# First attention: layout change of the outputs by transfers through DRAM in place of TensorE

## The chip, the cores and the metric
One NeuronCore of a Trainium2 chip runs the whole program, and the metric is the device time of one execution in microseconds (us). The engines are TensorE (PE; its weight loads are shown as PEld), VectorE (DVE), ScalarE (ACT), GpSimd (POOL) and SyncE (SP), which here issues transfers. Every engine works through its own queue in order. Engines meet only at semaphores. SP and ACT each have a DMA queue of their own; both feed the same 16 DMA engines.

## The reference, cut to what matters
The input is 16 sequences of 512 tokens with 128 channels. The network is: a mixture-of-experts block, softmax attention, the same mixture-of-experts block again, a second (kernel-feature) attention, and a spline block. The change touches the softmax attention alone, which for 16 heads of 8 channels computes

```
qkv  = x @ qkv_w + qkv_b                     # x is layer-normalised, 512 x 128
attn = softmax(q k^T / sqrt(8))              # 16 heads, 512 x 512 each
out  = (attn @ v) laid out as 512 x 128      # heads side by side
out  = out @ proj_w + proj_b                 # added to the residual
```

## The kernel before, in words
The program runs in stages with a barrier between them: set-up, `ffnA`, `att` (function `attn0`, the one changed), `ffnB`, another set-up, `att1k`, `att1q`. In `att` one sequence is a **batch** (16 batches). A batch has four **units** of four heads, and 32 **steps**, each of which handles one unit, one tile of 128 tokens and one pair of heads.

Every engine's program is a double loop: `m` over batches (18 turns, since work on a batch ends two turns after its scores began), and `n` over the 32 steps. What an engine does in step `n` stands in order in that loop. In each step TensorE does `again` (line 957: the scores of a step 42 steps back once more, transposed, with the row maxima folded in, two matmuls of 512 columns), `scores` (line 947: the scores of the next step, two matmuls), and on most steps `weigh` (line 969: eight matmuls of 256 columns by 32 columns of values, which accumulate in bank `o`). DVE takes the maxima of `scores` (line 698), ACT takes the exponential of `again` (line 873). Three double banks `pair` are handed round: `again` waits in `pair_free` for a maximum 1.5 steps old, `scores` for the exponential of the step before. The `scores` and `again` matmuls of one step lie on different rows of the array and can run at once.

Around that, one bank `misc` serves everything that is done once or a few times a batch, always in the order of `uses_of_misc`, each use waiting until the last one was read: the turned maxima, the turned input, the projections of queries, keys and values, and the outputs.

How the outputs leave. The values have a ninth column of ones, so a unit's bank `o` holds, for each of four heads, 8 rows of weighted sums and one row of softmax sums, tokens along the columns, in blocks of 32 rows. ACT copies it (`out`, line 879). TensorE turns it back (`turn_back`, line 117: four transposes into `misc`). DVE inverts the sums (line 720) and multiplies (line 722) into `otok`, which has tokens on partitions and heads side by side. When all four units of a batch are there, TensorE turns `otok` (`final`, line 111), ACT copies it to `ocol` (line 885), TensorE projects it (`projected`, line 993) and DVE adds it to the residual (`ended`, line 727). In turn `m` the units 2 and 3 of batch `m - 2` come at PE steps 7 and 15, `final` at 21, `projected` at 23, units 0 and 1 of batch `m - 1` at 25 and 30.

SP moves queries and keys to their spread layout through DRAM: `operands(m + 1)` waits until POOL has split the query into two parts (lines 770, 772), issues three writes (line 800), waits for them, reads 1 MB back (line 810), then does the same for the keys (line 816). Before that, in the same turn, `maxima(m - 1)` writes and reads the row maxima (lines 822, 825). POOL normalises a batch (lines 148, 154), adds the bias (line 786) and splits queries and keys, in that order, batch by batch.

Of the kernel before, what the change touches and what calls it, by code (L numbers as in the profile page):

```python
# [15 lines left out]
P = 128  # L16
# [549 lines left out]
HALF = 256  # L566
WEIGHED = {4: ((0, 0),), 5: ((0, 1),), 6: ((1, 0),), 7: ((1, 1),), 8: ((2, 0),), 9: ((2, 1), (3, 0)), 10: ((3, 1),)}
# [7 lines left out]
def attn0(nc, ctx, name, X, A, K, groups):  # L575
# [12 lines left out]
    (var, root, normed, biased, xT, xc, qp, kp, qr, kr, ql, kl, vp, vx, s_, mx, mt, mT, mr, t_, p_, w_, oT, oTT, on,  # L588
     fT, fc, fp, done) = signals(nc, ctx, name, "var root normed biased xT xc qp kp qr kr ql kl vp vx s mx mt mT mr t p w oT oTT"
                                 " on fT fc fp done")  # L590
# [14 lines left out]
    rec = mem.ring("rec", 2, [P, TILES, 4])  # L605
    otok = mem.ring("otok", 2, [P, GROUP])
# [5 lines left out]
    spread_m = nc.dram_tensor(name + "_spread_m", [4, BLOCK, GROUP], F32, kind="Internal").ap()  # L612
    xg = lambda b: X[:, b, :, :]
# [19 lines left out]
    def uses_of_misc():  # L633

        yield from (("x", 0), ("q", 0), ("k", 0), ("v", 0))
        for m in range(groups + 3):
# [5 lines left out]
            if old:  # L642
                yield "out", UNITS * (m - 2) + 2
            if new:
                yield "q", m + 1
                yield "k", m + 1
            if old:
                yield "out", UNITS * (m - 2) + 3
            if new:
                yield "v", m + 1  # L650
            if old:
                yield "final", m - 2
                yield "proj", m - 2
            if now:
                yield "out", UNITS * (m - 1)
                yield "out", UNITS * (m - 1) + 1
# [4 lines left out]
    def misc_free(pe, kind, k):  # L661
        n = misc_number[kind, k]
        if n:
# [11 lines left out]
            if kind == "out":  # L675
                pe.wait_ge(on, k + 1)
            if kind == "final":
                pe.wait_ge(fc, k + 1)
# [3 lines left out]
    def vector(v):  # L682
# [29 lines left out]
        def divided(w):  # L712
            b, u = divmod(w, UNITS)
            ov = misc[:, :].rearrange("p (t j r) -> p t j r", t=TILES, j=4)
            o = otok[b % 2][:, :].rearrange("p (t h d) -> p t h d", t=TILES, d=HDIM)
            rc = rec[w % 2]
            v.wait_ge(oTT, w + 1)
            if u == 0 and b >= 2:
                v.wait_ge(fT, b - 1)
            m = st.at(v.reciprocal(rc[:, :, :], ov[:, :, :, HDIM]))  # L720
            v.wait_ge(st.sem, m)
# [19 lines left out]
        for m in range(groups + 2):  # L741
            old, now = m >= 2, 1 <= m <= groups
            for n in range(STEPS):
# [12 lines left out]
                if n == 24 and old:  # L756
                    ended(m - 2)
# [1792 lines left out]
```

## Time and profile before

| | |
|---|---|
| runs of the kernel, us | 3351.72, 3384.48, 3382.59; median 3382.59 |
| profiled execution, us | 3352.73, with a span of 3350.8 from first to last instruction |
| mean granted TensorE clock | 0.921 of full |
| busy over the span | PE 88%, DVE 75%, ACT 53%, POOL 27% |
| stage `att` | about 440 to 1338 us; PE busy 823.69 of 898 us, DVE 684.18, ACT 593.71, POOL 147.23 |

The times of one instruction group in a row are busy time and the mean of one; for TensorE the two differ in meaning, since matmuls overlap: busy time is the union. "issue" as a cause of idle time means that the engine waited for nothing that the profile shows. A granted clock of 1.00 is 2.4 GHz and 0.50 is 1.2 GHz; a value between them is a stretch with both.

### The profile page before, as it was taken

The numbers are of one execution on the slowest core, as the hardware profiler recorded it, in microseconds if no ns is written. First come the engines' busy times: TensorE is split into PE (matmuls) and PEld (weight loads), VectorE is DVE, ScalarE is ACT, GpSimd is POOL, SyncE is SP. The second block draws the span as 40 slices with busy tenths as digits, with TensorE's granted clock in tenths as the row PEclk, the third lists the DMA queues.
The fourth block names the chain that finished last, engine by engine and source line by source line (L and its number), as shares of the span: only waits on it lengthen the run. The fifth ranks groups of instructions, "written<-read, shape, count | busy, mean of one in ns | idle before, by whom it ended". The sixth has DMA issues, their size and how long they took to land. (4 is left out here: it accounts for less than half of the span.)

```text
span 3350.8 us, 46737 instructions
## 1 busy us (share of the span) xinstructions
PE 2959.6 (88%) x16194; PEld 1788.4 (53%) x16194; DVE 2511.5 (75%) x6115; ACT 1760.6 (53%) x2683; POOL 904.5 (27%) x885
## 2 busy tenths in 40 slices
PE   7999969999999998899995689899799999989853
PEld 5666623443444433666664456566566666656432
DVE  6877768888888880788776797967467778787775
ACT  3444415777777775444435456455345555555544
POOL 2111022112112100211101345566323323343333
PEclk9999968999999996999995588999899999999975
DMA  2000022121222110100000000000000000000000
GB/s 76 1 1 1 1 88 86 70 93 68 81 93 78 72 49 5 51 1 1 1 1 0 1 7 19 13 20 26 32 13 13 13 7 13 13 7 26 7 7 25
DMA packets 33698, 99.03 MB, mean 30 GB/s; under 512 B 4184, under 2 KB 4792, under 8 KB 29240
## 3 DMA queue, kind: packets, MB, share of 16 engines
q1 hardware_dynamic: 31288, 91.85, 7.5%
q10 hardware_dynamic: 2176, 4.19, 0.3%
q8 instruction: 130, 2.13, 0.3%
q14 instruction: 104, 0.85, 0.1%
HBM read 53.56 MB, written 42.47 MB: 29 GB/s over the span
## 5 line engine op out<-in xcount | busy, mean ns | idle before, releaser
L698 DVE TENSOR_REDUCE att_mx<-att_pair 128x2 f32<-128x1024 f32 x512 | 616.8, 1219 | 124.4 <-PE att_pair L947 124.3
L873 ACT ACTIVATE att_pt<-att_pair 128x1024 f32<-128x1024 f32 x512 | 522.2, 1025 | 224.8 <-PE att_pair L957 222.7
L969 PE MATMUL att_o<-att_pt,att_vx 128*32 128x256 f32 x4096 | 327.8, 405 | 10.8 <-ACT att_oT L879 5.8
L947 PE MATMUL att_pair<-att_k,att_q 24*128 24x512 f32 x1024 | 267.5, 526 | 49.6 <-DMA att_k<-att_spread_k 14.0
L957 PE MATMUL att_pair<-att_q,att_k 26*128 26x512 f32 x1024 | 261.0, 510 | 0.0
L449 ACT ACTIVATE ffnA_h<-ffnA_up,b 128x512 f32<-128x512 f32 x144 | 99.0, 688 | 189.5 <-PE ffnA_up L105 186.0
L449 ACT ACTIVATE ffnB_h<-ffnB_up,b 128x512 f32<-128x512 f32 x144 | 99.0, 688 | 188.8 <-PE ffnB_up L105 183.6
L957 PEld LDWEIGHTS att_pair<-att_q,att_k 26*128 26x128 f32 x1024 | 96.9, 188 | 189.9 <-issue 164.1
L947 PEld LDWEIGHTS att_pair<-att_k,att_q 24*128 24x128 f32 x1024 | 98.8, 192 | 138.9 <-ACT att_pt L873 92.1
L969 PEld LDWEIGHTS att_o<-att_pt,att_vx 128*32 128x32 f32 x4096 | 90.6, 110 | 140.1 <-issue 118.6
L1889 ACT ACTIVATE att1k_sq<-att1k_k 128x512 f32<-128x512 f32 x128 | 76.2, 595 | 161.5 <-PE att1k_k L105 161.1
L148 POOL TENSOR_TENSOR ffnB_rstd<-ffnB_rstd,minus_half 128x4 f32<-128x4 f32 x16 | 16.5, 1029 | 454.7 <-DVE ffnB_rstd L264 454.7
L1956 PE MATMUL att1k_c<-att1k_feat,att1k_xn 128*128 128x512 f32 x256 | 132.2, 643 | 6.5 <-ACT att1k_ctx L1901 6.5
L2118 DVE TENSOR_REDUCE att1q_top<-att1q_wide 128x8 f32<-128x512 f32 x128 | 87.7, 685 | 64.1 <-PE att1q_wide L105 64.0
L2411 PE MATMUL att1q_acc<-att1q_qf,att1q_mem 128*128 128x512 f32 x256 | 132.3, 598 | 3.2 <-DVE att1q_qf L2156 3.2
L517 PE MATMUL ffnA_acc<-ffnA_hc,w 128*128 128x512 f32 x256 | 130.6, 592 | 0.0
L517 PE MATMUL ffnB_acc<-ffnB_hc,w 128*128 128x512 f32 x256 | 130.5, 591 | 0.0
L103 PE MATMUL ffnA_up<-ffnA_xh,w_hi 128*128 128x512 f32 x288 | 122.3, 425 | 0.5 <-DVE ffnA_h L360 0.4
L103 PE MATMUL ffnB_up<-ffnB_xh,w_hi 128*128 128x512 f32 x288 | 121.3, 421 | 0.8 <-DVE ffnB_h L360 0.4
L2282 ACT ACTIVATE att1q_qf<-att1q_half 128x512 f32<-128x512 f32 x128 | 75.8, 596 | 80.1 <-PE att1q_half L2380 80.0
L360 DVE SCALAR_TENSOR_TENSOR ffnA_h<-ffnA_up,b,ffnA_h 128x512 f32<-128x512 f32 x144 | 107.3, 745 | 13.8 <-ACT ffnA_h L449 11.4
L360 DVE SCALAR_TENSOR_TENSOR ffnB_h<-ffnB_up,b,ffnB_h 128x512 f32<-128x512 f32 x144 | 107.3, 745 | 13.7 <-ACT ffnB_h L449 11.3
(543 smaller groups left out, 7953.4 us busy)
## 6 DMA issues: line engine op xcount, KB each, us to landing
att_q<-att_spread_q SPq DMA_DIRECT2D x16, 1024.0 KB, 5.0
att_k<-att_spread_k SPq DMA_DIRECT2D x16, 1024.0 KB, 4.8
att_spread_q<-att_qhi SPq DMA_DIRECT2D x32, 256.0 KB, 2.5
att_spread_k<-att_khi SPq DMA_DIRECT2D x32, 256.0 KB, 3.3
context<-att1k_ctx SPq DMA_DIRECT2D x16, 512.0 KB, 2.6
att1q_cin<-context SPq DMA_DIRECT2D x16, 512.0 KB, 3.3
X<-L_attn_x ACTq DMA_DIRECT2D x8, 512.0 KB, 7.6
att_spread_q<-att_qlo SPq DMA_DIRECT2D x16, 256.0 KB, 2.5
```

Of the source, the lines that this page charges most:

```text
L103: pe.matmul(out, w[0], x[0], start=start, stop=False)
L360: v.scalar_tensor_tensor(h3[n % HELD][:, :], b3[:, :], W["b13"][:, 1, c:c + 1], s1[:, :], ALU.add, ALU.mult).then_inc(S.gl, 1)
L449: a.activation(h1[n % 4][:, :], up[2 * n % 4][:, :], ACT.Silu, bias=W["b13"][:, 0, c:c + 1]).then_inc(S.sil, 1)
L517: pe.matmul(acc[:, :], W["w2"][:, c, :], src[:, :], start=False, stop=c == CHUNKS - 1).then_inc(S.dn, 1)
L698: v.tensor_reduce(top[b % 2][:, t, h:h + 2], pair("s", k)[:, :].rearrange("p (h n) -> p h n", h=2), AX, ALU.max, negate=True).then_inc(mx, 1)
L873: a.activation(pt[k % 8][:, :, :].rearrange("p h n -> p (h n)"), pair("t", k)[:, :], ACT.Exp, scale=scale).then_inc(p_, 1)
L947: last = pe.matmul(pair("s", k)[:, (j - j0) * 512:(j - j0 + 1) * 512], qb[b % 3][r, u, t * P:(t + 1) * P], kb[b % 3][r, u, :], start=True, ...
L957: last = pe.matmul(pair("t", k)[:, (j - j0) * 512:(j - j0 + 1) * 512], kb[b % 3][r, u, t * P:(t + 1) * P], qb[b % 3][r, u, :], start=True, ...
L969: last = pe.matmul(obank[j * BLOCK:(j + 1) * BLOCK, cols], vxb[b % 3][:, t, 4 * u + j, :], pt[(2 * g + j // 2) % 8][:, j % 2, cols], start ...
L1956: last = pe.matmul(cb[:, cut], group(xn[i % 4][:, :])[:, t, :], feat[i % 2][:, t, cut], start=t == 0, stop=t == TILES - 1)
L2118: v.tensor_reduce(tp[:, t, side * 8:side * 8 + 8], heads_of(wide[wide_of("g", k)][:, :]), AX, ALU.max).then_inc(top, 1)
L2411: pe.matmul(acc[:, :], memb[i % 2][:, c, :], qfb[n % 12][:, :], start=c == 0, stop=c == PAIRS - 1).then_inc(gat, 1)
```

## The change: what it does
The four transposes a unit, the four transposes a batch, the copy to `ocol` by ACT and the eight DVE operations a batch go away. In their place:

- ACT, one step after it has copied a unit, issues a write of that 128 x 512 tile to a DRAM buffer `heads_o` (`kept`, steps 6, 14, 22, 30).
- SP reads the sixteen rows of sums as a 128 x 64 tile (`gathered`, pieces of 64 values) and the 128 rows of weighted sums as 128 x 512, heads side by side (`num`). This stands between the query part and the key part of `operands`.
- DVE inverts the 128 x 64 sums once a batch (`inverted`, step 19).
- SP, behind the read of the keys, writes the inverses to DRAM, waits, and reads them back with each head's row repeated eight times (`returned`).
- POOL multiplies (`divided`, 128 x 512), behind `spread` and ahead of the normalisation of the batch after next.
- TensorE's `projected` moves from step 23 to 26 and waits for POOL (`weighted`); DVE's `ended` moves from 24 to 28.

```diff
         def projected(b):
-            pe.wait_ge(fc, b + 1)
+            pe.wait_ge(weighted, b + 1)
...
-                if n == 21 and old:
-                    final(m - 2)
-                if n == 23 and old:
+                if n == 26 and old:
                     projected(m - 2)
-                if n == 25 and now:
-                    out(UNITS * (m - 1))
-                if n == 30 and now:
-                    out(UNITS * (m - 1) + 1)
```

```diff
+        def inverted(b):
+            v.wait_ge(dsum, 16 * (b + 1))
+            if b:
+                v.wait_ge(wr, 16 * b)
+            v.reciprocal(rec[:, :], sums[:, :]).then_inc(turned_over, 1)
...
+        def divided(b):
+            p.wait_ge(dnum, 16 * (b + 1))
+            p.wait_ge(drec, 16 * (b + 1))
+            if b:
+                p.wait_ge(fp, b)
+            p.tensor_tensor(ocol[:, :], num[:, :], recb[:, :], ALU.mult).then_inc(weighted, 1)
...
+        def gathered(b):
+            for written in wo:
+                sp.wait_ge(written, 16 * UNITS // 2 * (b + 1))
+            sp.dma_start(sums[:, :], heads_o[:, HDIM, :].rearrange("h (a n) -> h a n", n=FOLD)).then_inc(dsum, 16)
+            if b:
+                sp.wait_ge(weighted, b)
+            sp.dma_start(num[:, :], heads_o[:, 0:HDIM, :]).then_inc(dnum, 16)
+
+        def returned(b):
+            sp.wait_ge(turned_over, b + 1)
+            if b:
+                sp.wait_ge(drec, 16 * b)
+            sp.dma_start(spread_r.rearrange("h (a n) -> (h a) n", n=FOLD), rec[:, :]).then_inc(wr, 16)
+            sp.wait_ge(wr, 16 * (b + 1))
+            if b:
+                sp.wait_ge(weighted, b)
+            sp.dma_start(recb[:, :], spread_r.unsqueeze(1).to_broadcast([HEADS, HDIM, GROUP])).then_inc(drec, 16)
+
+        operands_q(0)
+        operands_k(0)
+        for m in range(groups + 2):
+            if 1 <= m <= groups:
+                maxima(m - 1)
+            if m + 1 < groups:
+                operands_q(m + 1)
+            if m >= 2:
+                gathered(m - 2)
+            if m + 1 < groups:
+                operands_k(m + 1)
+            if m >= 2:
+                returned(m - 2)
...
+        def kept(w):
+            b, u = divmod(w, UNITS)
+            a.wait_ge(oT, w + 1)
+            if u == 0 and b:
+                a.wait_ge(dsum, 16 * b)
+                a.wait_ge(dnum, 16 * b)
+            a.dma_start(heads_o[4 * u:4 * u + 4].rearrange("j r n -> (j r) n"), oTb[w % 2][:, :]).then_inc(wo[w % 2], 16)
```

## Rows read from the trace of the kernel before

**Rows 1.** Windows: us, busy PE PEld DVE ACT POOL (instructions), granted clock, DMA share, GB/s.

```profile
600.00:1200.00 600.00, 578.61 (x5160) 244.25 (x5158) 504.97 (x617) 441.13 (x504) 110.55 (x120) 0.99 0.22 81
755.00:760.00 5.00, 5.00 (x36) 1.89 (x32) 4.18 (x7) 2.35 (x3) 4.23 (x5) 0.50 0.00 0
```

**Rows 2.** Timeline, PE, two `again` two steps apart: start, us, engine, line.

```profile
960.69 0.50 PE L957 MATMUL att_pair<-att_q,att_k 26*128 26x512 f32 x2
...
963.31 0.50 PE L957 MATMUL att_pair<-att_q,att_k 26*128 26x512 f32 x2
```

**Rows 3.** Waits from 600 to 1200 us: waiter, releaser: total us, times, longest.

```profile
DVE att_mx L698 <- PE att_pair L947: 87.0, 230, 1.6
PEld att_pair L947 <- ACT att_pt L873: 73.6, 178, 0.6
```

**Rows 4.** Groups by form: count, then busy us, mean ns, idle us before.

```profile
L117 PE MATMUL att_misc<-ident,att_oT 128*128 128x128 f32 x256 | 44.6, 300 | 0.7 <-ACT att_oT L879 0.7
L111 PE MATMUL att_misc<-ident,att_otok 128*128 128x128 f32 x64 | 10.5, 286 | 0.8 <-DVE att_otok L722 0.8
L720 DVE RECIPROCAL att_rec<-att_misc 128x16 f32<-128x16 f32 x64 | 16.4, 256 | 60.1 <-PE att_misc L117 60.1
L885 ACT ACTIVATE att_ocol<-att_misc 128x512 f32<-128x512 f32 x16 | 9.5, 594 | 2.1 <-PE att_misc L111 2.1
L2139 DVE RECIPROCAL att1q_rec<-att1q_misc 128x64 f32<-128x64 f32 x16 | 8.7, 546 | 0.0
L772 POOL TENSOR_TENSOR att_klo<-att_kraw,att_khi 128x512 fp32r<-128x512 f32 x16 | 20.4, 1278 | 1.3
```

**Rows 5.** Timeline, POOL, the first operation of three normalisations, one a batch.

```profile
753.70 1.03 POOL L148 TENSOR_TENSOR att_rstd<-att_rstd,minus_half 128x4 f32<-128x4 f32 x1 [20.76 <-DVE att_rstd L692]
...
808.16 1.03 POOL L148 TENSOR_TENSOR att_rstd<-att_rstd,minus_half 128x4 f32<-128x4 f32 x1 [20.76 <-DVE att_rstd L692]
...
858.01 1.03 POOL L148 TENSOR_TENSOR att_rstd<-att_rstd,minus_half 128x4 f32<-128x4 f32 x1 [20.76 <-DVE att_rstd L692]
```

**Rows 6.** Timeline, SP's queue, in one batch: start, us of issuing.

```profile
917.74 0.33 SPq L822 DMA_DIRECT2D att_spread_m<-att_mrow  x1
...
942.95 0.35 SPq L816 DMA_DIRECT2D att_k<-att_spread_k  x1
```

**Rows 7.** Transfers: count, KB each, median us from issue to landing.

```profile
att_k<-att_spread_k SPq DMA_DIRECT2D x16, 1024.0 KB, 4.8
...
att_spread_m<-att_mrow SPq DMA_DIRECT2D x16, 256.0 KB, 2.0
...
raw_wk<-L_wk SPq DMA_DIRECT2D x1, 512.0 KB, 4.7
...
raw_w<-L_w SPq DMA_DIRECT2D x1, 256.0 KB, 5.1
```

**Rows 8.** Timeline of the same batch: steps 14, 19, 23 and 26.

```profile
934.23 0.68 ACT L851 ACTIVATE att_kraw<-att_misc,abqk 128x512 f32<-128x512 f32 x1
...
940.27 1.22 DVE L698 TENSOR_REDUCE att_mx<-att_pair 128x2 f32<-128x1024 f32 x1 [0.91 <-PE att_pair L947]
...
947.98 1.16 PE L993 MATMUL att_misc<-aproj,att_ocol 128*128 128x128 f32 x8
...
952.27 0.50 PE L957 MATMUL att_pair<-att_q,att_k 26*128 26x512 f32 x2
```

**Rows 9.** Timeline, PE, after gaps: end of `att`, and stage `att1q`.

```profile
1265.11 0.64 PE L969 MATMUL att_o<-att_pt,att_vx 128*32 128x256 f32 x8 [1.70 <-ACT att_oT L879]
...
1266.68 1.01 PE L117 MATMUL att_misc<-ident,att_oT 128*128 128x128 f32 x4
...
2754.61 1.12 PE L2432 MATMUL att1q_facc<-att1q_hid,tw 128*128 128x512 f32 x2 [1.75 <-DVE att1q_hid L2181]
```

**Rows 10.** Timeline, the last copy and the last addition of stage `att`.

```profile
1331.27 0.60 ACT L879 ACTIVATE att_oT<-att_o 128x512 f32<-128x512 f32 x1 [1.29 <-PE att_o L969]
...
1336.51 0.69 DVE L727 TENSOR_TENSOR X<-X,att_misc 128x512 f32<-128x512 f32 x1 [3.31 <-PE att_misc L993]
```

More of the change, by code:

```diff
@@ L786, in normal @@
             p.tensor_tensor(xg(b), xg(b), A["pb"][:, :].unsqueeze(1).to_broadcast([P, TILES, C]), ALU.add).then_inc(biased, 1)
-        for b in range(groups):
-            normal(b)
-            spread(b)
+        def divided(b):
[4 more added lines that the diff above has]
+            p.tensor_tensor(ocol[:, :], num[:, :], recb[:, :], ALU.mult).then_inc(weighted, 1)
+        normal(0)
+        spread(0)
+        if groups > 1:
+            normal(1)
+        for m in range(groups + 2):
+            if m + 1 < groups:
+                spread(m + 1)
+            if m >= 2:
+                divided(m - 2)
+            if m + 2 < groups:
+                normal(m + 2)
     def sync(sp):
@@ L900, in scalar @@
                     out(UNITS * (m - 2) + 2)
+                if n == 6 and old:
+                    kept(UNITS * (m - 2) + 2)
                 if n == 6 and new:
@@ L906, in scalar @@
                     out(UNITS * (m - 2) + 3)
+                if n == 14 and old:
+                    kept(UNITS * (m - 2) + 3)
                 if n == 14 and new:
@@ L912, in scalar @@
                     out(UNITS * (m - 1))
-                if n == 22 and old:
-                    final(m - 2)
+                if n == 22 and now:
+                    kept(UNITS * (m - 1))
                 if n == 29 and now:
                     out(UNITS * (m - 1) + 1)
+                if n == 30 and now:
+                    kept(UNITS * (m - 1) + 1)
     def tensor(pe):
@@ L977, in maxima @@
             last.then_inc(mT, 1)
-        def out(w):
-            pe.wait_ge(oT, w + 1)
-            misc_free(pe, "out", w)
-            turn_back(pe, misc, oTb[w % 2], ident).then_inc(oTT, 1)
-        def final(b):
-            pe.wait_ge(on, UNITS * (b + 1))
-            misc_free(pe, "final", b)
-            turn(pe, misc, group(otok[b % 2][:, :]), ident).then_inc(fT, 1)
         def projected(b):
-            pe.wait_ge(fc, b + 1)
+            pe.wait_ge(weighted, b + 1)
             misc_free(pe, "proj", b)
@@ L1016, in tensor @@
                     turned(m + 1)
-                if n == 7 and old:
-                    out(UNITS * (m - 2) + 2)
                 if n == 9 and new:
```

71 lines of the change are left out of this document (18 added, 53 removed).

## The prediction

> **What bounds the kernel now.** I read the windows first. In the steady part of `att` TensorE is busy 578.61 of 600 us at a clock of 0.99; DVE follows with 504.97, ACT with 441.13, POOL with 110.55 [rows 1]. So work taken from TensorE looks like time. The waits qualify that: DVE waits 87.0 us for `scores`, and the weight loads of `scores` wait 73.6 us, 178 times, for ACT's exponential [rows 3]. Part of TensorE's busy time is two matmul pairs done one after the other which could have run at once. The timeline shows it: two plain steps take 963.31 - 960.69 = 2.62 us [rows 2], in one of which the pairs overlap (about 1.0) and in the other of which `scores` comes late (about 1.6). A plain step costs 1.31 on average. A batch takes 858.01 - 808.16 = 49.85 us, but one took 808.16 - 753.70 = 54.46 [rows 5]: there the clock was 0.50 for a while [rows 1]. Such a half-clock spell costs 4.6 us.
>
> **Removed.** A batch loses sixteen transposes of a unit (44.6 / 16 = 2.79 us busy) and four of `final` (10.5 / 16 = 0.66) [rows 4]: 3.45 us of union, or five groups of which each pushes the next step back by about 0.58. It isn't all time. A group behind an overlapping step fills the wait for ACT and lets the next step overlap too: it costs 1.58 - 1.31 = 0.27. Behind a late step it costs the full 0.58. The mean, 0.42, times five is 2.1 us a batch; the upper bound is 2.9.
>
> **Added on ACT.** Four issues a batch; the nearest row, the same tile shape written to DRAM by SP, took 0.33 us to issue [rows 6], so 1.3 us, against a copy of 0.59 saved [rows 4]. ACT is busy 74% [rows 1], but it is the engine `scores` waits for, and issues at steps 6 and 14 stand next to two other copies. Cost between 0 and 0.7 a batch; I take 0.1, since the copy saved and the step given up to `projected` cover it elsewhere. That leaves 2.0 us a batch (1.4 to 2.9).
>
> **DVE and POOL.** DVE loses four inversions (256 ns each) with their products, and gets one of 128 x 64, for which another stage's row has 546 ns [rows 4]. That is a gain on an engine with slack, hence nothing. POOL gets 1.28 us [rows 4] on an engine busy 18%; it stands ahead of a normalisation whose input comes only at step 29, so it is hidden unless it ends after that.
>
> **The new waits.** *DVE, step 19.* If the sums are late, the last 12 maxima of the batch queue behind it. Unit 3 is stored after step 14 (934.2) and lands after 2.0 us, perhaps 3 beside the read of the queries. The sums' read then stands behind that read in the queue. I put its landing at about 939.9. DVE ends its step-19 maximum at 940.27 + 1.22 = 941.5 [rows 8], 0.3 earlier after the change. Cover about 1.3 us; no wait taken.
>
> *TensorE, step 26.* Before, the read of the keys was issued 942.95 - 934.23 = 8.72 us after the copy of the keys began [rows 6, 8]. Now 288 KB of reads stand ahead of the key writes. By the rows for 1024 and 256 KB each further 256 KB takes (4.8 - 2.0) / 3 = 0.93 [rows 7], so the read goes out at about 944.0. The write of the inverses is issued behind it. Does it wait for it? A read of 256 KB, issued behind a queue of 512 KB ones, took 5.1 us, later than the 4.7 of the one ahead, although 256 KB alone takes 2.0 [rows 7]: the queue serves in order. So it lands with the keys, at 944.0 + 4.8 = 948.8; the repeated read, 256 KB, takes 2.0 to 2.5 (the only repeating read before stands behind others, so its own time isn't seen), to 951.1; the product and two signals 1.4, to 952.5. On the other side, TensorE before was at step 26 at 952.27 [rows 8]. With `projected` gone from step 23 (1.09) and three groups fewer since step 14 (1.1) it is there at 950.1, and asks for the product behind that step's work, at 951.4. **A wait of 1.1 to 1.3 us**; between none (the write isn't held up, or steps go slower) and 2.5 (a slow repeated read). While it waits, every `again`, `scores` and `weigh` queues behind it, so DVE and ACT run dry. Over 14 steady batches: 14 x 2.0 = 28 us gained, 14 x 1.2 = 17 given back.
>
> *End of the stage.* Before, from the last copy to the last addition it took 1337.20 - 1331.27 = 5.9 us [rows 10]. Now four hops (unit, sums, inverses, repeated inverses) at 2.0 to 2.3 make 8.3, and with copy 0.6, inversion 0.5, product 1.3, projection and addition 2.4 (1.7 at half clock, 0.7) and signals 0.6 this is 13.7: +7.8. Against it go the last turns' groups, about 1.0 each at half clock [rows 9], of seven some half on the path: -3.8. Net +4.
>
> **The sum** is -28 + 17 + 4 = -7 us, on 3352.73 for the profiled execution: 3346. The three runs have their median 29.9 above that execution, at 3382.59, so I forecast 3376 for the median. The excess would be six or seven half-clock spells at 4.6, which is an estimate and not shown.
>
> **Rivals.**
>
> *The transfers come in time.* If the small write passes the read of the keys, the product is there by about 950 and nothing waits: -28 + 4 = -24, or with 2.9 a batch -37: 3359 to 3346. For: DMA engines are busy only 22% [rows 1]. Against: the order of landings [rows 7]. Chance 0.20.
>
> *The clock holds better without the transposes.* In the end part the fall shows first in a group of transposes [rows 9]. If they are what lets the clock fall, the spell in the profiled execution and the excess of the median go: 3346 - 5 = 3341, and with no wait either 3324. Against: the batches of 49.85 us had the same groups, at full clock [rows 5]. Chance 0.20. The Trainium skill ("TensorE: Matmul & The Clock Gate", Part 4: PE-mode transpose) says that work in transpose mode doesn't count as busy for the clock as other matmuls do; by that rule this rival is what would happen. The trace only fits it, one spell being too few.
>
> *The wait brings the clock down in every batch* (slower). Its place is step 26, its price 4.6 us a spell on top of the wait [rows 5], and it decides from about 1.7 us of idle: in the end of `att` the clock fell within 1.6 us after an idle time of 1.70 [rows 9]. If each batch has it, 14 x 4.6 = 64: 3376 + 64 = 3440; in half of them 3408; with a wait of 2.5 us 3458. Against: in `att1q` idle times of 1.75 us left the clock full, after full-width matmuls [rows 9], and my wait is shorter. Chance 0.25. The Trainium skill ("TensorE: Matmul & The Clock Gate", HAM oscillation) tells of a kernel whose clock fell at each wait for a transfer; it speaks against this change, if the wait is long enough.
>
> *Forecast*, short wait, clock as before: 0.35.
>
> **The numbers.** One per cent is 34 us, about what a measurement of this kernel can tell from no change. Faster by more: the clock rival 0.20, half of the first rival and more 0.12, the forecast's edge 0.03, together 0.35. Slower: 0.25. Within: 0.40. The range leaves out the fastest corner of the clock rival and the case of a spell in every batch with a long wait: 3322 to 3435. The forecast's own range is 3350 to 3395.
>
> **What would show it.** Right: a batch period of about 49.0 us; in the waits TensorE's L993 group waits 1.2 us a batch for POOL; POOL's product waits for the repeated read; SP's write of the inverses takes nearly 5 us to land; DVE's inversion waits for nothing. Wrong: the product idle for TensorE's sake (wait zero), a period under 48 (each group worth its full 0.58), DVE waiting at step 19, or steady windows at 0.50 behind step 26 in most batches. The end of the stage, last copy to last addition, should be some 14 us.

## The result, and the profile after

The changed kernel takes 3443.77 us (median of 4 runs, 3435.60 to 3458.07) against 3382.02 for the kernel before on the same chip: a ratio of 1.0207, with a 95% interval of 1.0159 to 1.0254. By the medians it is slower by 62 us, by the ratio by 70. Ratios here and below pair runs made side by side and leave out those more than 1.5% above the fastest of their kernel, so they can differ by up to 0.3% from what the medians give. The prediction was 3376 with a range of 3322 to 3435; the result lies above the range, next to the 3440 of the third rival.

The page of the changed kernel, whose profiled run took 3448.59 us with a span of 3446.8: the busy row of TensorE, and the granted clock in 40 slices of the span.

```profile
PE 3038.8 (88%) x15874; PEld 1803.4 (52%) x15874; DVE 2493.0 (72%) x6003; ACT 1756.6 (51%) x2667; POOL 925.5 (27%) x901
...
PEclk9999957888787886699997588989899999999975
```

The sixth to the seventeenth slice are the stage `att`. Its digits are 5 to 8. Before the change this line was `PEclk9999968999999996999995588999899999999975`, with nines in the steady part of the stage. The mean granted clock is 0.872 where it was 0.921. At the end of `att` this run was 82.2 us behind the profiled one of before (1419.39 against 1337.20 us), and at its end 96.0: the stages behind `att`, which the change doesn't touch, took 2027.4 us against 2013.6.

The steady part of `att` in the changed kernel, same columns as [rows 1]:

```profile
600.00:1200.00 600.00, 573.12 (x4496) 228.31 (x4496) 448.93 (x489) 398.26 (x446) 115.50 (x121) 0.82 0.29 102
```

TensorE is busy as long as in [rows 1], with 4496 matmuls where 5160 were. Its clock is 0.82 where it was 0.99. The same busy share holds less work, since each instruction takes longer. So "busy" alone would have hidden the loss; the clock beside it shows it.

The batch period, by POOL's normalisation in two successive batches of the changed kernel (the reading of [rows 5]):

```profile
937.91 1.03 POOL L148 TENSOR_TENSOR att_rstd<-att_rstd,minus_half 128x4 f32<-128x4 f32 x1 [6.41 <-DVE att_rstd L683]
995.08 1.03 POOL L148 TENSOR_TENSOR att_rstd<-att_rstd,minus_half 128x4 f32<-128x4 f32 x1 [7.32 <-DVE att_rstd L683]
```

This batch took 57.17 us. Over the steady batches the mean is 54.33, against 49.83 before. At microsecond resolution the changed kernel spent 266 of 706 steady us at half clock, in 19 spells; the kernel before spent 37 of 648, in two. The first of these spells, at least 23 us at the start of the stretch (509 us), is in every kernel of this study. The thirteen batches of the stretch account for 706.3 - 647.8 = 58.5 us. With 15.3 more in the turns between it and the last copy, and 8.4 more at the end of the stage (below), that makes the 82.2. The medians differ by less, 62 us, since the profiled run of before is 29 us below its median, and that of the changed kernel 5 us above.

What waits in that stretch, total us, times, longest:

```profile
ACT att_pt L894 <- PE att_pair L986: 199.7, 230, 5.4
DVE att_mx L689 <- PE att_pair L976: 148.3, 230, 5.0
...
PEld att_misc L1012 <- POOL att_ocol L772: 19.8, 11, 3.6
...
PE att_misc L1012 <- POOL att_ocol L772: 11.4, 7, 3.1
...
DVE att_rec L707 <- DMA att_sums<-att_heads_o: 1.0, 2, 0.8
```

The new wait of TensorE for the product (L1012 for POOL's L772) is 11.4 us in 600, about one us a batch. DVE, which waited 87.0 us for `scores` in [rows 3], now waits 148.3 for them, and ACT waits 199.7 us for `again`, 158.3 before. Both are starved by a slower TensorE.

Which came first, the wait or the fall of the clock? The projection of five batches shows it (start, us, what it waited for):

```profile
931.55 1.16 PE L1012 MATMUL att_misc<-aproj,att_ocol 128*128 128x128 f32 x8 [2.57 <-POOL att_ocol L772]
987.81 2.07 PE L1012 MATMUL att_misc<-aproj,att_ocol 128*128 128x128 f32 x8
1043.08 1.16 PE L1012 MATMUL att_misc<-aproj,att_ocol 128*128 128x128 f32 x8 [1.73 <-POOL att_ocol L772]
1098.11 2.08 PE L1012 MATMUL att_misc<-aproj,att_ocol 128*128 128x128 f32 x8 [1.15 <-POOL att_ocol L772]
...
1210.39 1.16 PE L1012 MATMUL att_misc<-aproj,att_ocol 128*128 128x128 f32 x8 [1.69 <-POOL att_ocol L772]
```

A projection of 1.16 us ran at full clock, one of 2.07 at half. Of the twelve from 605 to 1211 us, four began at full clock (a fourth, at 713.81, took 1.77 us and is not shown). They had waited 1.69 to 3.12 us, and a half-clock spell began within 6 us of each (at 714, 933, 1049 and 1216). The other eight found the clock already down: it had fallen 6 to 9 us ahead of them, when TensorE had been busy for 4.56 to 4.69 of the last 5 us. Of these eight, four waited, for 0.24 to 1.74 us, and four not at all. So the clock goes down at two places in a batch, and only four falls in twelve batches come at the wait. That the wait brought on these four is argued from the order alone.

The more frequent one, in the batch of 937.91 to 995.08. Two windows of the changed kernel, columns as above, and TensorE's timeline across the fall:

```profile
975.00:980.00 5.00, 4.56 (x46) 1.88 (x46) 4.69 (x9) 4.38 (x6) 0.00 (x0) 1.00 0.60 193
980.00:985.00 5.00, 5.00 (x40) 1.78 (x36) 3.80 (x6) 2.69 (x4) 0.00 (x0) 0.54 0.67 249
```

```profile
976.88 0.64 PE L998 MATMUL att_o<-att_pt,att_vx 128*32 128x256 f32 x8
977.45 0.50 PE L986 MATMUL att_pair<-att_q,att_k 26*128 26x512 f32 x2
978.06 0.50 PE L976 MATMUL att_pair<-att_k,att_q 24*128 24x512 f32 x2
978.39 0.45 PE L986 MATMUL att_pair<-att_q,att_k 26*128 26x512 f32 x2
979.07 0.49 PE L976 MATMUL att_pair<-att_k,att_q 24*128 24x512 f32 x2 [0.22 <-ACT att_pt L894]
979.65 0.64 PE L998 MATMUL att_o<-att_pt,att_vx 128*32 128x256 f32 x8
980.22 0.64 PE L986 MATMUL att_pair<-att_q,att_k 26*128 26x512 f32 x2
980.47 0.79 PE L976 MATMUL att_pair<-att_k,att_q 24*128 24x512 f32 x2
```

From 980.2 us on the pairs of matmuls of 512 columns go from 0.50 us to 0.64 and then 0.79. The one idle time that the timeline names there is 0.22 us, in all TensorE was idle for 0.44 of the 5 us before, and the product (986.49) is still 6 us away. The fall comes between steps 22 and 23, just behind step 21, in which nothing is weighed and at whose end `final` stood before the change. The one spell of the kernel before in its steady part (755 us) also began behind a step in which nothing is weighed.

The chain that makes the product, in the same batch, from the read of the keys on (start, us to issue or run):

```profile
977.74 0.35 SPq L812 DMA_DIRECT2D att_k<-att_spread_k  x1
978.19 0.37 SPq L835 DMA_DIRECT2D att_spread_r<-att_rec  x1
983.26 0.56 SPq L839 DMA_DIRECT2D att_recb<-att_spread_r  x1
```

```profile
986.49 1.27 POOL L772 TENSOR_TENSOR att_ocol<-att_num,att_recb 128x512 f32<-128x512 f32 x1 [15.22 <-issue]
```

The write of the inverses (978.19) had landed when 983.26 went out, 5 us later. The transfers of the stage in the changed kernel, median us from issue to landing:

```profile
att_k<-att_spread_k SPq DMA_DIRECT2D x16, 1024.0 KB, 5.2
att_heads_o<-att_oT ACTq DMA_DIRECT2D x64, 256.0 KB, 2.0
...
att_recb<-att_spread_r SPq DMA_DIRECT2D x16, 256.0 KB, 3.2
...
att_spread_r<-att_rec SPq DMA_DIRECT2D x16, 32.0 KB, 4.9
```

The end of the stage in the changed kernel, from the last copy to the last addition (against [rows 10]):

```profile
1405.08 0.60 ACT L900 ACTIVATE att_oT<-att_o 128x512 f32<-128x512 f32 x1 [2.25 <-PE att_o L998]
...
1409.87 0.55 DVE L707 RECIPROCAL att_rec<-att_sums 128x64 f32<-128x64 f32 x1 [34.17 <-DMA att_sums<-att_heads_o]
...
1412.06 0.52 SPq L839 DMA_DIRECT2D att_recb<-att_spread_r  x1
1415.27 1.26 POOL L772 TENSOR_TENSOR att_ocol<-att_num,att_recb 128x512 f32<-128x512 f32 x1 [54.27 <-DMA att_recb<-att_spread_r]
...
1418.70 0.69 DVE L712 TENSOR_TENSOR X<-X,att_misc 128x512 f32<-128x512 f32 x1 [8.27 <-PE att_misc L1012]
```

That is 1419.39 - 1405.08 = 14.3 us, where it was 5.9.

### The profile page after: what moved, and what is told of

It reads as the page before. It is cut to its first block and busy times, and to the rows that moved or that the text cites. A ratio compares the mean times of both kernels' runs of the same rounds, so it can differ in the third digit from the quotient of the medians.

```text
span 3446.8 us, 46096 instructions
## 1 busy us (share of the span) xinstructions
PE 3038.8 (88%) x15874; PEld 1803.4 (52%) x15874; DVE 2493.0 (72%) x6003; ACT 1756.6 (51%) x2667; POOL 925.5 (27%) x901
## 5 line engine op out<-in xcount | busy, mean ns | idle before, releaser
L998 PE MATMUL att_o<-att_pt,att_vx 128*32 128x256 f32 x4096 | 397.1, 481 | 11.6 <-ACT att_oT L900 6.8
L976 PE MATMUL att_pair<-att_k,att_q 24*128 24x512 f32 x1024 | 304.8, 600 | 43.1 <-DMA att_k<-att_spread_k 14.0
L986 PE MATMUL att_pair<-att_q,att_k 26*128 26x512 f32 x1024 | 298.7, 587 | 0.9 <-DVE att_mx L689 0.6
L986 PEld LDWEIGHTS att_pair<-att_q,att_k 26*128 26x128 f32 x1024 | 109.6, 214 | 254.5 <-issue 192.9
L998 PEld LDWEIGHTS att_o<-att_pt,att_vx 128*32 128x32 f32 x4096 | 99.8, 122 | 174.3 <-issue 156.3
L976 PEld LDWEIGHTS att_pair<-att_k,att_q 24*128 24x128 f32 x1024 | 111.7, 217 | 116.9 <-ACT att_pt L894 67.1
L1965 PE MATMUL att1k_c<-att1k_feat,att1k_xn 128*128 128x512 f32 x256 | 142.4, 686 | 6.8 <-ACT att1k_ctx L1910 6.8
L360 DVE SCALAR_TENSOR_TENSOR ffnA_h<-ffnA_up,b,ffnA_h 128x512 f32<-128x512 f32 x144 | 107.3, 745 | 13.8 <-ACT ffnA_h L449 11.4
L1832 DVE TENSOR_REDUCE att1k_diag<-att1k_sq 128x16 f32<-128x1024 f32 x64 | 77.4, 1209 | 54.8 <-ACT att1k_sq L1898 54.8
```

The lines of the kernel that those rows point to most:

```text
L360: v.scalar_tensor_tensor(h3[n % HELD][:, :], b3[:, :], W["b13"][:, 1, c:c + 1], s1[:, :], ALU.add, ALU.mult).then_inc(S.gl, 1)
L976: last = pe.matmul(pair("s", k)[:, (j - j0) * 512:(j - j0 + 1) * 512], qb[b % 3][r, u, t * P:(t + 1) * P], kb[b % 3][r, u, :], start=True, ...
L986: last = pe.matmul(pair("t", k)[:, (j - j0) * 512:(j - j0 + 1) * 512], kb[b % 3][r, u, t * P:(t + 1) * P], qb[b % 3][r, u, :], start=True, ...
L998: last = pe.matmul(obank[j * BLOCK:(j + 1) * BLOCK, cols], vxb[b % 3][:, t, 4 * u + j, :], pt[(2 * g + j // 2) % 8][:, j % 2, cols], start ...
L1965: last = pe.matmul(cb[:, cut], group(xn[i % 4][:, :])[:, t, :], feat[i % 2][:, t, cut], start=t == 0, stop=t == TILES - 1)
```

## The experiments

The theory after the result: the change removes real work from TensorE, and its loss is the granted clock. The rivals were that the wait for the product brings the clock down, and that the missing groups of transposes do so by themselves. Beside the time, each experiment is read by the mean granted clock over all its timed runs. Over the 25 runs of the kernel before in the first group of experiments, time and clock go together (correlation -0.98), with 28 us for each 0.01 of clock. That price comes from one kernel; on others it is an estimate. "Half" is the time at half clock in the steady stretch of the one profiled run, the 23 us or more at its start included.

| kernel | median us (runs) | before, same chip | ratio, 95% interval | mean clock | batch, us | half, us |
|---|---|---|---|---|---|---|
| before | 3382.29 (25) | | | 0.9086 | 49.83 | 37 |
| changed | 3443.77 (4) | 3382.02 | 1.0207 [1.0159, 1.0254] | 0.8752 | 54.33 | 266 |
| 1 five groups put back | 3420.79 (10) | 3382.29 | 1.0134 [1.0090, 1.0178] | 0.9006 | 52.14 | 90 |
| 2 late projection | 3377.34 (10) | 3382.29 | 0.9986 [0.9953, 1.0019] | 0.8953 | 50.98 | 177 |
| 3 one group at step 21 | 3433.18 (4) | 3382.29 | 1.0127 [1.0066, 1.0188] | 0.8862 | 53.31 | 173 |
| 4 before, one transpose a group | 3396.42 (10) | 3382.29 | 1.0041 [1.0012, 1.0070] | 0.8934 | 51.54 | 157 |
| 5 inverses first | 3406.83 (10) | 3386.89 | 1.0066 [1.0039, 1.0094] | 0.8832 | 51.67 | 204 |
| 6 late, five groups | 3370.13 (10) | 3386.89 | 0.9967 [0.9937, 0.9998] | 0.9141 | 49.29 | 30 |
| 7 late, five groups of matmuls | 3386.87 (10) | 3386.89 | 0.9999 [0.9968, 1.0031] | 0.9087 | 50.78 | 78 |
| 8 before, held | 3404.71 (10) | 3386.89 | 1.0057 [1.0027, 1.0088] | 0.9065 | 51.51 | 71 |
| 9 late, groups at 21 and 25 | 3387.96 (12) | 3375.05 | 1.0051 [1.0022, 1.0079] | 0.8994 | 49.67 | 78 |
| 10 late, groups at 21, 25, 29 | 3364.25 (12) | 3375.05 | 0.9971 [0.9941, 1.0000] | 0.9073 | 49.06 | 57 |
| 11 inverses first, late | 3381.93 (10) | 3375.05 | 1.0024 [0.9991, 1.0057] | 0.8945 | 50.25 | 144 |
| 12 same as 6 | 3368.44 (12) | 3375.05 | 1.0005 [0.9979, 1.0031] | 0.9148 | 49.08 | 23 |

The kernel before stood at 0.9079 of clock beside experiments 5 to 8, and at 0.9107 beside 9 to 12, and its own median differs by 12 us between them. So kernels of different groups are compared by their ratios and by the distance of their clock to that of before: 0.001 of ratio is 3.4 us. The changed kernel was run with its own comparison, ahead of the experiments; its clock is set against 0.9086.

**1. Put the TensorE work back and keep all the rest.** Five groups of four transposes of the identity into `misc`, at the steps where the old ones stood. Nothing reads them.

```diff
+        def filled(n, m):
+            misc_free(pe, f"fill{n}", m)
+            for t in range(TILES):
+                last = pe.transpose(misc[:, t * P:(t + 1) * P], ident[:, :], ident[:, :])
...
+                if n in (7, 15, 21, 25,) and (now if n == 25 else old):
+                    filled(n, m)
...
+                if n == 30 and now:
+                    filled(n, m)
```

> The changed kernel, with five groups of four transposes (of the identity, into the spare bank, read by nobody) put back at TensorE's steps 7, 15, 21, 25 and 30, where the groups that the change removed stood. Theory 'thin steps': the groups kept TensorE's clock up, and without them it falls by itself, wait or no wait. Then the spells of 1.2 GHz nearly vanish and the time comes to that of the kernel before plus the longer end of the stage, 3360 to 3395 us, clock above 0.91. Theory 'wait': the clock falls because TensorE waits for GpSimd's product at step 26. The groups delay step 26 by some 2 us and so shorten that wait, so this theory too allows a gain, but only if the wait goes; if a wait of over 0.5 us is left in most batches, it expects 3410 us or more. Rival 'DMA route': the transfers or ScalarE's issues cost the time; then it is 3440 us or more, since they are all still there and work is added.

More work on TensorE made the kernel faster by 23 us, with the clock up from 0.8752 to 0.9006 and half-clock time down from 266 to 90 us. The intervals of the two ratios overlap a little; the clocks don't (0.870 to 0.880 in the runs of the changed kernel, 0.893 to 0.907 here). The wait stayed, all of it on TensorE:

```profile
PE att_misc L1029 <- POOL att_ocol L784: 15.9, 12, 3.0
```

So the missing groups cost clock, and the wait costs something too: 3420.79 isn't yet 3382. The time is in the range of the theory 'wait', the clock between the two theories. In this trace all twelve projections are reached at full clock: the fall ahead of them is gone. Seven spells begin at the projection or within 7 us behind it, after waits of 3.01, 2.70, 1.87, 1.26, 1.07, 0.31 and 0.21 us, and none after 2.05 and 1.53. So the length of the wait alone doesn't tell whether the clock falls.

**2. Take the wait away and leave the groups out.** The projection goes to step 30 and its addition to 31, when the product has long been there.

```diff
-                if n == 26 and old:
+                if n == 30 and old:
                     projected(m - 2)
...
-                if n == 28 and old:
+                if n == 31 and old:
                     ended(m - 2)
```

> The changed kernel with the projection moved from TensorE's step 26 to 30 and the addition from VectorE's step 28 to 31, so that the product is long there and nothing waits for it. No filler. Theory 'wait': spells vanish, batches take about 48 us, 3340 to 3375 us. Theory 'thin steps': only the wait itself goes (about 1 us a batch, 14 us), the half-clock spells stay: 3410 to 3440 us, clock below 0.90. Rival 'DMA route': 3430 us or more.

By the ratios a gain of 75 us on the changed kernel (1.0207 to 0.9986), to the level of before. The wait is gone (0.2 us in the stretch). The clock isn't back: 0.8953. The window of this kernel, and its normalisations in a part that no spell touches:

```profile
600.00:1150.00 550.00, 527.81 (x4510) 215.16 (x4502) 454.69 (x494) 401.18 (x450) 115.88 (x121) 0.92 0.32 112
```

```profile
722.10 1.03 POOL L148 TENSOR_TENSOR att_rstd<-att_rstd,minus_half 128x4 f32<-128x4 f32 x1 [1.06 <-DVE att_rstd L683]
769.63 1.03 POOL L148 TENSOR_TENSOR att_rstd<-att_rstd,minus_half 128x4 f32<-128x4 f32 x1 [1.42 <-DVE att_rstd L683]
817.14 1.03 POOL L148 TENSOR_TENSOR att_rstd<-att_rstd,minus_half 128x4 f32<-128x4 f32 x1 [2.26 <-DVE att_rstd L683]
```

An undisturbed batch takes 47.5 us, 2.3 less than the 49.85 of before: the gain of the work is real. It is given back in spells, 177 us at half clock. The result fits neither theory whole: the time is 2 us above the range of 'wait', the clock in that of 'thin steps'.

**3. One group alone, at step 21**, since the fall in the trace above came at that place.

```diff
+                if n in (21,) and (now if n == 25 else old):
+                    filled(n, m)
```

> The changed kernel with one group of four transposes put back, at step 21, the step of a batch in which nothing is weighed and after which the traced clock fell in the batch read closely. 0.58 us of work a batch, 9 us in all, is added. Theory 'thin steps': this is the thinnest place, so at least a third of the half-clock time goes, 3370 to 3420 us. Theory 'wait': the wait shortens by at most 0.6 us, spells at step 26 stay, 3420 to 3450 us.

The time, 3433.18, is in the range of the theory 'wait', and 18 spells stayed. But the half-clock time went from 266 to 173 us and the mean clock from 0.8752 to 0.8862, and what is left has moved. The wait on TensorE and the fall in one batch, in windows of one us:

```profile
PE att_misc L1021 <- POOL att_ocol L776: 29.6, 11, 4.4
```

```profile
980.00:981.00 1.00, 0.47 (x8) 0.00 (x0) 1.00 (x2) 0.85 (x1) 0.00 (x0) 1.00 0.00 0
981.00:982.00 1.00, 0.00 (x0) 0.00 (x0) 0.18 (x1) 0.00 (x0) 0.00 (x0) 0.63 0.77 252
```

In none of the twelve batches from 590 to 1210 us did the clock fall ahead of the wait any more, where it had in eight. In eleven of them it fell during the wait or within 3 us behind it. TensorE now comes to the projection at full clock, so earlier, and waits longer: 29.6 us from 600 to 1200, where it was 11.4. So the group holds the clock at its own place, and the clock then falls at the wait. That puts some of the loss on the wait, though in experiment 1 the clock held behind a wait of 2.05 us.

**4. Leave the transposes out of the kernel before**, with no transfer, wait or place changed. One transpose in each group stays. The three others of each are left out, and so the output is another one; DVE reads a constant tile in their place, and ACT's copy reads `otok`.

```diff
-            turn_back(pe, misc, oTb[w % 2], ident).then_inc(oTT, 1)
+            pe.transpose(misc[:, 0:P], oTb[w % 2][:, 0:P], ident[:, :]).then_inc(oTT, 1)
...
-            turn(pe, misc, group(otok[b % 2][:, :]), ident).then_inc(fT, 1)
+            pe.transpose(misc[:, 0:P], otok[b % 2][:, 0:P], ident[:, :]).then_inc(fT, 1)
```

> The kernel before, with no transfer and no new wait, but with one transpose in place of four in each group that turns a unit or a batch (5 groups a batch, so 15 of 20 transposes gone). It leaves out the turning: VectorE's division reads a tile of ones and ScalarE's copy reads the undivided-layout tile, so the attention's output is another one; the instructions and sizes elsewhere stay. Theory 'thin steps': the clock falls here too, although nothing waits for a transfer: 3390 us or more, clock below 0.90. Theory 'wait': the clock stays as in the kernel before and the time falls by 15 to 30 us below it.

Fifteen transposes fewer a batch, and the kernel got slower by 0.4% (interval 0.1 to 0.7%). Its normalisations show both halves of it, columns as before:

```profile
867.48 1.03 POOL L148 TENSOR_TENSOR att_rstd<-att_rstd,minus_half 128x4 f32<-128x4 f32 x1 [19.87 <-DVE att_rstd L693]
921.62 1.03 POOL L148 TENSOR_TENSOR att_rstd<-att_rstd,minus_half 128x4 f32<-128x4 f32 x1 [21.13 <-DVE att_rstd L693]
969.91 1.03 POOL L148 TENSOR_TENSOR att_rstd<-att_rstd,minus_half 128x4 f32<-128x4 f32 x1 [19.86 <-DVE att_rstd L693]
```

One batch takes 48.3 us, 1.5 less than before, and the next 54.1, with spells in it. The clock is 0.8934 against 0.9086. Time and clock are in the ranges of 'thin steps'. This is the cleanest run of the study: the DRAM path isn't there, and the clock falls all the same. It isn't quite clean: from the other tiles DVE's product took 391 ns where it took 291, and ACT's copy 642 where it took 594.

**5. Write and read the inverses ahead of the read of the keys.** Nothing else in SP's queue or elsewhere moves.

```diff
             write(spread_k, (khb, klb, khb), wk)
+
+        def operands_k_back(b):
             sp.wait_ge(wk, 16 * PRODUCTS * (b + 1))
...
             if m >= 2:
                 returned(m - 2)
+            if m + 1 < groups:
+                operands_k_back(m + 1)
```

> The changed kernel, its projection still at TensorE's step 26, but on SyncE's queue the write and the repeated read of the inverses stand ahead of the 1 MB read of the keys instead of behind it. If the chain was late because the small write stood behind that read, its time from issue to landing falls from 4.9 us to 2.0 to 2.5, the product comes some 3 us sooner, TensorE waits for it in no batch, and the time is that of the kernel with the late projection: 3365 to 3390 us. Rival 'the write is slow by itself' (pieces of 256 bytes): it lands in over 4 us again, the wait stays, 3420 us or more. Rival 'the place': at step 26 the projection costs more than at 30 even without a wait: 3395 to 3420 us.

The transfers of this kernel, and its window:

```profile
att_k<-att_spread_k SPq DMA_DIRECT2D x16, 1024.0 KB, 5.9
...
att_spread_r<-att_rec SPq DMA_DIRECT2D x16, 32.0 KB, 2.1
```

```profile
600.00:1150.00 550.00, 536.15 (x4302) 216.76 (x4300) 429.07 (x474) 381.70 (x429) 110.24 (x116) 0.84 0.30 105
```

The 32 KB write lands after 2.1 us instead of 4.9, so its delay was the read ahead of it in the queue. TensorE waits for the product no more, with the projection still at step 26. By the ratios that gained 48 us on the changed kernel. The clock is still 0.0247 below that of before, where the changed kernel was 0.0334 below: most of the fall needs no wait. The median is 17 us above the range that was expected and in that of the rival 'the place'. In eleven of twelve batches from 590 to 1180 us the clock fell 6 to 8 us ahead of the projection, here in the batch whose projection begins at 697.08:

```profile
690.00:691.00 1.00, 1.00 (x11) 0.48 (x12) 1.00 (x2) 0.76 (x2) 0.00 (x0) 0.92 1.10 186
691.00:692.00 1.00, 1.00 (x12) 0.29 (x4) 1.00 (x2) 0.52 (x1) 0.71 (x1) 0.50 0.77 311
```

**6. The projection late and the five groups back.** Neither wait nor lighter TensorE.

```diff
+                if n in (7, 15, 21, 25, 29) and (now if n in (25, 29) else old):
+                    filled(n, m)
+                if n == 30 and old:
                     projected(m - 2)
```

> The kernel with the late projection (step 30, no wait), with five groups of four transposes of the identity a batch put back at steps 7, 15, 21, 25 and 29. Theory 'two causes': what was lost to the clock has two parts, the thinner TensorE and the wait. With no wait and the groups back, the clock comes to that of the kernel before (0.905 to 0.912 against 0.895 for the late projection alone), and since the groups' own work is back too, the time is 3380 to 3400 us, the kernel before plus 8 us for the longer end of the stage. Theory 'wait alone': the clock stays at 0.895 and the time goes up by the work added, 3400 us or more.

```profile
600.00:1150.00 550.00, 527.12 (x4784) 222.69 (x4776) 461.22 (x497) 405.27 (x453) 116.48 (x122) 0.99 0.32 114
```

```profile
904.58 1.03 POOL L148 TENSOR_TENSOR att_rstd<-att_rstd,minus_half 128x4 f32<-128x4 f32 x1 [3.68 <-DVE att_rstd L694]
954.11 1.03 POOL L148 TENSOR_TENSOR att_rstd<-att_rstd,minus_half 128x4 f32<-128x4 f32 x1 [3.23 <-DVE att_rstd L694]
```

The clock is 0.99 in the stretch, as in [rows 1], and 0.9141 in the mean of the runs. The batch takes 49.5 us, 2.0 more than in experiment 2 and nearly that of before. The groups cost what the prediction said (2.1), and the clock that they hold pays for it: 0.9967 against 0.9986 for experiment 2, with intervals that overlap. Time and clock are both better than the 3380 to 3400 us and 0.905 to 0.912 that were expected, and the DRAM path is all there: it doesn't by itself cost the clock.

**7. The same with two ordinary matmuls in place of the four transposes of each group**, to see whether transposes are special.

```diff
-                last = pe.transpose(misc[:, t * P:(t + 1) * P], ident[:, :], ident[:, :])
+                if t < 2: last = pe.matmul(misc[:, t * P:(t + 1) * P], ident[:, :], ident[:, :], start=True, stop=True)
```

> The same, but each group is two ordinary 128 x 128 matmuls (0.58 us) in place of four transposes. If transposes count less for the clock than other matmuls do, the clock is higher than with the transposes, by 0.005 or more, and the time lower by 10 us or more. If any work counts that fills the gaps, clock and time agree with the run with transposes within 0.003 and 8 us.

The clock is 0.9087: better than with nothing (0.8953), a little worse than with transposes (0.9141), by 0.0054 and 17 us. Neither of the two expectations had that. The two sorts of filler differ in number and length too, so no more than this follows: transposes hold the clock at least as well.

**8. A wait alone, in the kernel before.** POOL does a product on a spare tile when the weighing of step 26 is done, and TensorE waits for it at step 26.

```diff
+        def hold(m):
+            p.wait_ge(w_, marks[m])
+            p.tensor_tensor(spare[:, :], spare[:, :], spare[:, :], ALU.mult).then_inc(held, 1)
...
+                if n == 26 and m in turns:
+                    pe.wait_ge(held, turns.index(m) + 1)
```

> The kernel before, all transposes kept and no transfer added, but at step 26 of turns 2 to 15 TensorE waits for one GpSimd product of 128 x 512 (1.28 us), on a tile that nobody uses, which GpSimd begins when that step's weighing is done: an idle time of about 1.4 us a batch and nothing else. Theory 'two causes': the wait also brings the clock down a little, by 0.005 to 0.012 from 0.909, so the time is 14 x 1.4 = 20 us for the waits and 10 to 30 us for the clock above the kernel before: 3412 to 3432 us. If the wait costs only itself, 3397 to 3407 us. If each wait brings a full spell of 4.6 us, 3450 us or more.

```profile
PE att_pair L978 <- POOL att_spare L802: 14.5, 12, 1.2
```

14.5 us of wait in the stretch, 1.2 in each of twelve batches, cost 17.8 us by the medians (14 x 1.2 = 17) and 9 to 30 by the interval of the ratio. The mean clock barely moved: 0.9065 against 0.9079. In the trace a half-clock spell began within 6 us behind four of the twelve waits. By the means over the runs, though, a wait of the length that I predicted, with the transposes there, costs about its own length.

**9, 10, 12. How few groups are enough?** The late kernel with groups at 21 and 25, with 21, 25 and 29, and experiment 6 once more. The edits are shown against experiment 6.

```diff
-                if n in (7, 15, 21, 25, 29) and (now if n in (25, 29) else old):
+                if n in (21, 25,) and (now if n == 25 else old):
```

```diff
-                if n in (7, 15, 21, 25, 29) and (now if n in (25, 29) else old):
+                if n in (21, 25, 29) and (now if n in (25, 29) else old):
```

> The kernel with the late projection (step 30, no wait) and only two groups of four identity transposes a batch, at steps 21 and 25, in the stretch between the values' projection (17) and the outputs' (30) in which TensorE does nothing but the pairs and the weighing. If the clock is held by filling that stretch, it comes to 0.905 or more with 0.9 us a batch less work than with five groups: 3350 to 3370 us, below the kernel before. If the whole batch has to be filled, the clock stays near 0.897 and the time near that of the late projection alone, 3375 to 3395 us.

> The same with a third group at step 29. Held by filling the stretch from 17 to 2: clock 0.910 or more, 3352 to 3372 us. If the whole batch counts, halfway between the late projection alone and the run with five groups in clock, 0.903 to 0.908, and 3370 to 3385 us.

> The kernel with late projection and five groups of identity transposes once more, with more rounds, since its interval against the kernel before ended at 0.9998. If it is faster, the ratio is 0.993 to 0.999 again, the median 3360 to 3378 us and the clock 0.912 to 0.916; if that was chance, the ratio's interval takes in 1 and the clock is at 0.909.

Two groups: 3387.96 at 0.8994, about as if the whole batch had to be filled. The third, at step 29, brings 24 us and 0.0079 of clock. All five bring the clock to 0.9148 but no time (3368.44 against 3364.25), since each group costs its work. Experiment 10 has the lowest median of the study, 0.9971 of before with an interval that ends at 1.0000; experiment 6 had 0.9967 and its repetition 1.0005. None beats the kernel before by an amount that these runs settle.

**11. Experiments 5 and 2 together**: the inverses first, the projection at step 30 and the addition at 31 (shown against experiment 5).

```diff
-                if n == 28 and old:
+                if n == 31 and old:
                     ended(m - 2)
...
-                if n == 26 and old:
+                if n == 30 and old:
                     projected(m - 2)
```

> The inverses' transfers ahead of the read of the keys, as in the run before, and the projection at step 30 as in the late one. The run with the inverses first and the projection at 26 had no wait and still took 29 us more than the late projection, so one of two things costs that: the place of the projection or the order on SyncE's queue. If it is the place (26 or 30), this takes 3370 to 3385 us and has a clock of 0.895. If it is the order of the transfers, 3400 us or more, with 0.883.

1.0024 of before, with the clock 0.0162 below it, both as expected if the place is what counts. Experiment 2, with SP's old order, had 0.9986 and 0.0133: close, with intervals that overlap. Experiment 5, which waits for nothing either and has the projection at step 26, had 1.0066 and 0.0247. By that the place of the projection is worth some 14 us, through the clock, though these intervals overlap as well (from 1.0039 there, to 1.0057 here). Whether the place matters, and why, stays open.

## Why the prediction was wrong

Seen from the changed kernel, three steps lead back to the clock of before. "Clock" is the distance of the mean clock to that of before beside it; the us are differences of the ratios, taken of 3380 us.

| from | to | what differs | clock | us |
|---|---|---|---|---|
| changed | 5 | no wait for the product | -0.0334 to -0.0247 | -48 |
| 5 | 11 | projection at 30, not 26 | -0.0247 to -0.0162 | -14 |
| 11 | 12 | five groups back, SP's order back | -0.0162 to +0.0041 | -6 |

The first step holds the waits themselves, 13.1 us in twelve batches. The last adds 28 us of work (14 x 2.0) and is still no slower. The missing groups are the largest part of the fall: 0.020 here and between experiments 2 and 6, and 0.025 from the changed kernel to experiment 1. By 28 us for each 0.01 that is 56 to 70 us, against 33 us of work saved (14 x 2.35). This is an estimate and looks high: from experiment 2 to 6 the same price gives 55 us won for 28 of work, and the ratios differ by 6 us. The steps don't simply add: without the groups a wait and a place count for more than the wait of experiment 8 did with them.

Point by point:

- **Removed work, 2.0 us a batch (1.4 to 2.9).** Right within its bounds: an undisturbed batch of experiment 2 takes 47.5 against 49.85, a gain of 2.3 with all additions on ACT, DVE and POOL in it.
- **DVE at step 19, no wait.** Right: 1.0 us in the whole stretch.
- **The small write queues behind the read of the keys.** Right: 4.9 us, and 2.1 when it goes first.
- **The repeated read, 2.0 to 2.5.** Mis-sized: 3.2, some 1 us more, which is about what the wait at full clock was longer. I had 1.1 to 1.3 us. In the four batches where TensorE came to the projection at full clock it waited 1.69, 1.73, 2.57 and 3.12. In the others, slowed already, it waited 0 to 1.74. The mean over twelve, 13.1 / 12 = 1.1, is the number forecast, and for another reason. The condition that the third rival named, 1.7 us of idle, was met in those four batches, and the clock fell after each. It isn't a sufficient one, nor a needed one: in experiment 1 the clock held after 2.05 us and fell after 0.21.
- **End of the stage, 13.7 us.** Right: 14.3. Of the 3.8 us set against it (seven groups at about 1.0, half of them, give 3.5) no run shows by itself whether they arrived.
What in the profile of before could have told? The median of its runs, 29.9 us above the profiled one. I read it as six or seven spells and set it aside as an estimate. It was right in kind: the runs of before differ by up to 72 us, between 3346.6 and 3418.8, and their mean clock goes with it. What makes a spell come in one run and not in the next, no run shows. But where it happens, a change of TensorE's load must be priced in clock too, in both directions.

## What to carry to other kernels

Where the same kernel's runs differ by a per cent, and the granted clock explains the difference, suspect that TensorE falls to half clock easily. In this kernel, taking small matmuls away cost as much as they took, or more: try it with a filler put back before believing in either the gain or the loss. Price a chain of transfers at its longest row, not its shortest, when an engine waits at its end: here one row was 1 us too short. Read where in the batch a spell begins, and not only how many there are: in experiment 3 the falls at one place went and others came. A small transfer issued behind a large one in a queue was here about as late as the large one (4.9 and 5.2 us); put the small one first.

## What the runs showed of the hardware

- The clock fell with TensorE almost always busy, 4.56 of the last 5 us: at 980.2 us, after matmuls of 24 and 26 rows, 512 columns, and value matmuls into 32 columns, with one named idle time of 0.22 us. Four transposes of 0.66 us put at step 21 (experiment 3) kept it from falling there in twelve of twelve batches. Leaving out 15 of 20 transposes in a batch of 49.85 us (experiment 4) lowered the mean clock from 0.9086 to 0.8934.
- In the runs of before, 0.01 of mean clock is 28 us of 3382, and time and clock go together (correlation -0.98).
- A read of 256 KB that takes each row of 2 KB eight times from DRAM landed after 3.2 us (3.3 and 3.4 in other kernels), where a plain write of 256 KB (`heads_o`) took 2.0. No run has a plain read of that size with nothing ahead of it in the queue.
- A wait of 1.2 us in each batch, in a kernel with its transposes, cost 17.8 us in all and left the mean clock where it was, within 0.0014. In experiment 3, where the waits were 1.3 to 4.4 us, the clock fell at eleven of twelve.
- A write of 32 KB landed after 4.9 us behind a read of 1 MB in the same queue, and after 2.1 us ahead of it.
